# Layer 1 of a two-layer transformer kernel: the experts of the mixture run on their own tokens in 64 sorted tiles instead of on all tokens

## The reference

```python
def _L1_attn_ref(x, ...):            # 16 heads, 128 score features (64 plain, 64 with rope), 128 value features
    scores = g * sem_scores + (1.0 - g) * geo_scores
    attn = jax.nn.softmax(where(causal, scores, NEG_INF), axis=-1)      # 1024 x 1024 per head
    return einsum('bhqk,bkhd->bqhd', attn, v).reshape(b, sl, H * DV) @ wo

def _L1_ffn_ref(hidden_states, ...):
    topk_w, topk_idx = jax.lax.top_k(softmax(x @ gate_w.T), 4)          # 4 of 32 experts for each token
    comb = zeros((T, 32)).at[arange(T)[:, None], topk_idx].add(topk_w / sum(topk_w))
    out0 = sigmoid(x @ shared_expert_gate_w.T) * (silu(x @ sg.T) * (x @ su.T)) @ sd.T   # 512 hidden
    def body(acc, inp):                                                  # for each of the 32 experts
        gu = x @ gu_w.T                                                  # 2 * 96 hidden
        h = silu(gu[:, :96]) * gu[:, 96:]
        return acc + w_e[:, None] * (h @ dn_w.T), None
```

## Time and profile before

| | us |
|---|---|
| median of 3 runs (1105.45 to 1122.83) | 1106.43 |
| the profiled execution, its own time | 1106.36 |
| its span, first to last instruction | 1104.6 |
| layer 1 from its first instruction, 308.4, to the end | 796.2 |
| transposes of head 0 to transposes of head 15 | 680.9 |
| mean granted TensorE clock, share of full speed | 0.929 |

### The profile page before, as it was taken

One profiled execution on the slowest core, in us unless ns is written; L12 is line 12 of the kernel. 1 busy time (PEld: TensorE's weight loads), 2 busy tenths in 40 slices (PEclk: granted clock), 3 DMA queues, 4 the chain that ended last, 5 costly groups with the idle time before them and its releaser, 6 DMA issues.

```text
span 1104.6 us, 15520 instructions
## 1 busy us (share of the span) xinstructions
PE 988.5 (89%) x5701; PEld 753.1 (68%) x5701; DVE 792.2 (72%) x1338; ACT 477.2 (43%) x981; POOL 401.8 (36%) x352
## 2 busy tenths in 40 slices
PE   4797999977777879999999999999999999999996
PEld 3684544533644758787787787777878778777775
DVE  5687555630558568868968868877896896987883
ACT  3322554553232344444544535545444453453552
POOL 2430000010034344635525535454463452544441
PEclk9895588786889989999999999999999999999999
DMA  5630121100030210200200020020020020001000
GB/s 223 229 88 1 31 60 31 32 1 1 21 110 16 60 46 10 68 25 1 56 22 25 11 67 25 10 67 25 11 67 25 1 52 25 25 10 49 15 1 38
DMA packets 19452, 46.41 MB, mean 42 GB/s; under 512 B 3033, under 2 KB 4705, under 8 KB 19105
## 3 DMA queue, kind: packets, MB, share of 16 engines
q1 hardware_dynamic: 19376, 45.43, 13.6%
HBM read 37.81 MB, written 7.61 MB: 41 GB/s over the span
## 4 chain that ended last, share of the span: by engine, by line
PE 50%; DVE 16%; issue 3%; DMA 1%; ACT 1%; POOL 0%; SPq 0%; DVEq 0%; ACTq 0%
PE bank L1535 15%; PE bank L1571 10%; PE bank L1662 8%; PE bank L1581 8%; PE bank L1639 4%; PE bank L1557 4%; DVE d_pT_lo L1421 3%; DVE d_swap L1281 2%; DVE d_swap L1283 2%; DVE d_g_act L1260 1%; DVE d_neg_max L1308 1%; DVE d_rot L1281 1%; DVE d_rot L1296 1%; DVE d_g_act L1256 1%; DMA d_vw_raw<-in_w_v 1%
## 5 line engine op out<-in xcount | busy, mean ns | idle before, releaser
L1471 POOL TENSOR_SCALAR d_probs<-d_probs,d_row_inv 128x1024 f32<-128x1024 f32 (+7 forms) x128 | 101.4, 794 | 227.0 <-DVE d_row_inv L1313 226.5
L1160 ACT ACTIVATE d_probs<-bank,d_neg_max 128x1024 f32<-128x1024 f32 (+7 forms) x128 | 95.5, 746 | 96.5 <-DVE d_neg_max L1308 93.9
L598 DVE TENSOR_REDUCE b_maxes<-bank 128x2 f32<-128x1024 f32 (+2 forms) x96 | 89.5, 956 | 37.3 <-PE bank L626 20.4
L1421 DVE TENSOR_TENSOR d_pT_lo<-bank,d_pT_hi 128x512 fp32r<-128x512 f32 x192 | 98.5, 547 | 21.1 <-ACT d_pT_hi L1217 13.6
L1217 ACT CAST d_pT_hi<-bank 128x512 fp32r<-128x512 f32 x192 | 84.9, 483 | 65.7 <-PE bank L1639 65.0
L1535 PE MATMUL bank<-xT_hi,d_gu_hi 128*128 128x512 f32 x224 | 97.0, 433 | 9.8 <-DVE d_g_act L1256 5.6
L1308 DVE TENSOR_REDUCE d_neg_max<-bank 128x1 f32<-128x1024 f32 (+7 forms) x128 | 95.1, 748 | 11.3 <-PE bank L1584 11.1
L1639 PE MATMUL bank<-ident,d_probs 128*128 128x128 f32 x576 | 83.0, 277 | 17.7 <-DVE d_pT_lo L1421 15.9
L575 ACT ACTIVATE b_probsT<-bank 128x512 f32<-128x512 f32 x140 | 76.0, 593 | 48.6 <-PE bank L626 40.2
L1535 PE MATMUL bank<-xT_hi,d_gu_lo 128*128 128x512 f32 x224 | 90.5, 404 | 0.0
L1535 PE MATMUL bank<-xT_lo,d_gu_hi 128*128 128x512 f32 x224 | 90.4, 403 | 0.0
(11 more groups left out here) (238 smaller groups left out, 2544.9 us busy)
## 6 DMA issues: line engine op xcount, KB each, us to landing
gu_raw<-in_gu SPq DMA_DIRECT2D x24, 256.0 KB, 2.6
d_cb<-comb_scratch SPq DMA_DIRECT2D x9, 512.0 KB
qk_raw<-in_w_qk SPq DMA_DIRECT2D x16, 256.0 KB, 6.3
d_ow_raw<-in_ow_b SPq DMA_DIRECT2D x8, 384.0 KB, 3.2
q_stack<-a_part_hi SPq DMA_DIRECT2D x4, 512.0 KB, 5.4
k_stack<-a_part_hi SPq DMA_DIRECT2D x4, 512.0 KB, 5.1
d_vw_raw<-in_w_v SPq DMA_DIRECT2D x8, 256.0 KB, 10.3
d_ow_raw<-in_ow_a SPq DMA_DIRECT2D x8, 256.0 KB, 10.2
```

The source lines that it names most:

```text
L598: nc.vector.tensor_reduce(maxes[:, p % 2, c, :, i], bank[:, first:first + 2, 0:w], AX_X, ALU.max, negate=True).then_inc(maxed, 1)
L1160: nc.scalar.activation(probs[s % NP_][:, 0:width(s)], score_bank(s, width(s)), ACT.Exp, bias=neg_max[:, h.col(s)], accum_out=row_sum[:, h. ...
L1421: nc.vector.tensor_tensor(pT_lo[c][:, j:j + blocks, col:col + P], bank[:, T_BANK + tu % 2, 0:blocks * P].rearrange("p (b q) -> p b q", b=b ...
L1471: nc.gpsimd.tensor_scalar(probs[s % NP_][:, 0:width(s)], probs[s % NP_][:, 0:width(s)], row_inv[:, h.col(s)], 1.0, ALU.mult, ALU.mult).the ...
```

## The change

**Experts.** Each token has 4 experts, so there are 4096 pairs of token and expert, called slots here. Slots are sorted by expert, each expert's padded to whole tiles of 128, in 64 tiles (`XTILES`) of which each belongs to one expert. `rank` on PE and a longer routing on DVE (18 pieces, `routes`) compute the slot of each token and the expert of each tile. POOL scatters the normed token rows into a memory buffer (`x_slots`, 8192 rows) with 32 indirect DMAs of 128 rows. Two tiles at a time (`PAIRS` = 32) then go through four units: `X` turns the rows (4 transposes), `G` is gate and up (12 matmuls of 192 columns), `H` turns the hidden tile (2 transposes), `Y` is down (6 matmuls of 256 columns). DVE steps of a pair are `xlo`, two for the gate, `hlo`, `yout`; results go to `y_slots` in memory. At the end POOL gathers them with 32 more indirect DMAs, and DVE adds them with their weights (`combine`). Weights of a tile's expert (`ew`, 128 x 640) are loaded by SP, which reads the expert's number from memory into a register first (`value_load`), and are split by ACT and POOL.

**Layout.** `acc` has tokens on the partitions. An output unit is two token tiles of 3 matmuls of 256 columns. `join_layer0` no longer turns `x` or the gate, and stores the normed rows (`x_normed`, 1 MB). `x_slots` (8 MB) is cleared in `project_layer0` by 8 DMAs of 1 MB on SP's queue, behind the loads of the first pair of heads and ahead of those of pairs 1 and 2.

**Shared feed-forward and routing.** They move from the prologue into heads 0 and 1 as units `sg` (gate, up) and `so` (down). The prologue keeps `qk` and `v` of the first heads and two score tiles. Heads 2 to 14 hold the 32 pairs: 3 in each even head but head 2, which has 2, and 2 in each odd head. Head 15 holds none.

**Order.** A class `Plan` replaces the lists. It puts the fillers (`sg`, `so`, `rank` or `X G H Y`) evenly between the steps of `ORDER` by its own costs and gives every PE step a time; the steps of DVE, ACT, POOL and SP are sorted by such times plus fixed lags. The numbers in it are the program's own and nothing measured here.

```diff
@@ -279,6 +290,11 @@
+            sp.wait_ge(zeroed, 1)
+            slots = scratch["x_slots"].rearrange("(n p r) d -> n p r d", n=CLEARS, p=P)
+            for n in range(CLEARS):
+                sp.dma_start(slots[n], zeros.rearrange("p (o d) -> p o d", o=1).to_broadcast([P, NT, D])
+                             ).then_inc(early["cleared"], 16)
...
+            sp.wait_ge(norm.step, norm.DONE + NT)
+            sp.dma_start(scratch["x_normed"].rearrange("(j p) d -> p j d", p=P), xn[:]).then_inc(xn_stored, 16)
+            sp.wait_ge(xn_stored, 16)
...
+class Plan:
...
+    FILL = {1: (0.0, 0.8), 2: (0.3, 1.0)}
+    ORDER = ("T0 S2 S3 T1 S4 T2 S5 qk0 S6 T3 S7 qk1 T4 qk2 T5 pv0 qk3 T6 T7 S8 pv1 S9 "
+             "out0 v0 out1 v1 out2 v2 out3 v3")
...
+        return {"qk": 1.4, "v": 1.44, "out": 0.72, "sg": 1.4, "so": 1.44, "rank": 1.0, "X": 0.45, "G": 1.2, "H": 0.23,
+                "Y": 0.75}[name]
...
+    def fillers(self, h):
+
+        if h < 2:
+            pairs = [("sg", (p, part)) for p in range(4 * h, 4 * h + 4) for part in range(2)]
+            outs = [("so", (h, n)) for n in range(OUT_UNITS)]
+            return pairs[:6] + ([("rank", ())] if h == 0 else []) + pairs[6:] + outs
+        return [(name, (q,)) for q in EXPERT_PAIRS[h] for name in "XGHY"]
...
+            while k < len(fill) and done >= (first + (last_at - first) * (k + 0.3) / len(fill)) * total:
+                self.add(*fill[k])
+                k += 1
+            self.add(*step)
+            done += self.cost(*step)
...
-    PE_ORDER = [
-        "T0 S2 pair0 S3 T1 S4 pair1 T2 S5 qk0 S6 S7 T3 pair2 qk1 T4 T5 qk2 pv0 qk3 T6 T7 S8 pv1 S9 "
-        "out0 out1 out2 out3",
-        "T0 S2 S3 pair0 T1 pair1 S4 S5 qk0 T2 S6 pair2 T3 S7 qk1 qk2 T4 T5 pv0 T6 qk3 T7 S8 pv1 "
-        "out0 v0 v1 S9 v2 out1 out2 v3 out3",
-    ]
...
+    def expert_steps(lead):
+
+        free = END("so", 1, OUT_UNITS - 1) + 13.2 - lead
+        return [(max(START("G", i // 2) - lead + 2 * (i % 2), free + 1.2 * i), "ew", (i,)) for i in range(2 * NQ)]
...
+    dve_order = ordered(
+        after("S", 0.1, "max") + after("S", 2.6, "inv") + after("T", 0.7, "tlo") + after("qk", 0.1, "rope")
+        + after("v", 0.8, "vlo") + after("pv", 0.8, "pvlo") + after("out", 0.1, "oadd") + after("so", 0.1, "soadd")
+        + [(t + 0.3, "spair", (at[0],)) for t, _, at in after("sg", 0, "") if at[1] == 1]
+        + after("X", 0.8, "xlo") + after("G", 0.7, "gate") + after("H", 0.6, "hlo") + after("Y", 0.1, "yout")
+        + [(ROUTE_AT + ROUTE_GAP * n if n < 7 else max(ROUTE_AT + ROUTE_GAP * n, END("rank") + 0.1 + 1e-3 * n)
+            if n < 13 else END("rank") + ROUTE_GAP * (n - 12), "route", n) for n in range(ROUTE_FUNCS)]
+        + [(COMBINE_AT + 6 + 3.2 * j, "combine", j) for j in range(NT)])
...
+                + expert_steps(13)
+                + [(max(t, END("so", 1, OUT_UNITS - 1) + 1 + 2 * at[0]), name, at) for t, name, at in ahead("X", 8, "xs")] + after("Y", 1.0, "ystore")
+                + [(COMBINE_AT + 100 + n, "store", j) for n, j in enumerate(STORED)])
...
+                    i = at[0]
+                    if i == 0:
+                        sp.wait_ge(unit_done, done("so", 1, OUT_UNITS - 1))
+                        sp.wait_ge(scattered, NT * TOPK * 16)
+                    if i >= 2:
+                        sp.wait_ge(ew_hi_done, i - 1)
+                        sp.wait_ge(ew_lo_done, i - 1)
+                    e = sp.value_load(scratch["slot_expert"][0:1, i:i + 1], min_val=0, max_val=NE - 1)
+                    sp.dma_start(ew_raw[i % 2], d["ew"][bass.ds(e, 1)].rearrange("o p n -> (o p) n")
+                                 ).then_inc(ew_in[i % 2], 16)
...
+                    j = at
+                    dve.wait_ge(gathered[j], TOPK * 16)
+                    for k in range(TOPK):
+                        dve.wait_ge(acc_done, acc_at[name, at] + k)
+                        nc.vector.scalar_tensor_tensor(acc[:, j, :], yk[:, (j % NYK) * TOPK + k, :], top_w[:, j, k:k + 1],
+                                                       acc[:, j, :], ALU.mult, ALU.add).then_inc(acc_done, 1)
+                    dve.wait_ge(acc_done, acc_at[name, at] + TOPK)
+                    nc.vector.sem_inc(combined)
...
+                elif name == "scatter":
+                    j = at // TOPK
+                    if at == 0:
+                        pool.wait_ge(xn_in, 16)
+                        pool.wait_ge(route_step, SLOT_STEP + 1)
+                        pool.wait_ge(early["cleared"], CLEARS * 16)
+                    nc.gpsimd.indirect_dma_start(scratch["x_slots"], bass.IndirectOffsetOnAxis(slot_u[:, at:at + 1], 0),
+                                                 xn[:, j, :], None).then_inc(scattered, 16)
+                else:
+                    j, k = at // TOPK, at % TOPK
+                    if at == 0:
+                        for i in range(2):
+                            pool.wait_ge(y_stored[i], 16 * (NQ // 2))
+                    if k == 0 and j >= NYK:
+                        pool.wait_ge(combined, j - NYK + 1)
+                    nc.gpsimd.indirect_dma_start(yk[:, (j % NYK) * TOPK + k, :], None, scratch["y_slots"],
+                                                 bass.IndirectOffsetOnAxis(slot_u[:, at:at + 1], 0)
+                                                 ).then_inc(gathered[j], 16)
...
+                elif name == "G":
+                    q = at[0]
+                    pe.wait_ge(unit_free, freed("X", q))
+                    pe.wait_ge(ew_lo_done, 2 * q + 2)
+                    for a in range(2):
+                        out = unit_bank(u)[:, a * GW:(a + 1) * GW]
+                        for k in range(KT):
+                            slots = slice((k * 2 + a) * P, (k * 2 + a + 1) * P)
+                            cols = slice(k * GW, (k + 1) * GW)
+                            hi, lo = ew_hi[q % 2][:, a, cols], ew_lo[q % 2][:, a, cols]
+                            for n, (m, w) in enumerate(three((xs_hi[:, slots], hi), (xs_lo[:, slots], hi),
+                                                             (xs_hi[:, slots], lo))):
+                                last = nc.tensor.matmul(out, m, w, start=(k == 0 and n == 0),
+                                                        stop=(k == KT - 1 and n == 2))
```

1434 lines of the change are left out of this document (777 added, 657 removed), and 8 rows, old and new, of tables (ACT_ORDER, DVE_ORDER).

## The result

| | before | after |
|---|---|---|
| median, us | 1105.94 (4 runs, 1102.66 to 1122.83) | 1206.71 (4 runs, 1203.57 to 1222.29) |
| ratio | | 1.091 (95% interval 1.087 to 1.095) |
| span of the profiled execution | 1104.6 | 1205.3 |
| first transposes (T0) of head 0, from the span's start | 381.7 | 341.1 |
| heads 0 and 1 | 100.8 | 151.0 |

The account below looks back on a forecast made before the run. PE was taken to set the rate, DVE next, with DVE setting each head's first part. Prologue −45.7, heads 0 and 1 +15.6, heads 2 to 14 −15, tail +12, layer 0 0: −33, so 1073 us (−3.0%), range 1025 to 1118.

Parts of the forecast that it names:

- 64.4 stay: Heads 2 to 14: removing the old experts' 25.2 us of PE from a round of 89.6 leaves 64.4.
- DVE loses three pairs, 7.2, so 15.4 stay: Even head, T0 to pv0: removing three old expert pairs' DVE steps shortens this part from 22.6 us to 15.4.
- the third rope ahead of pv0: Even heads: with G between qk2 and pv0, pv0 waits for the third rope, +3.5 us; T0 to pv0 stays 22.8.
- Price of a pair: Heads 2 to 14: each pair of expert tiles adds 2.97 us on PE, 0.2 of it for a type change.
- Waits of 2 to 2.3 us: Second part of a head, after pv0: pairs' units add waits of 2.3 us in even heads, 2 in odd ones.
- Heads 0 and 1: Shared feed-forward, routing and scatters moved here: head 0 +6.4, head 1 +3.3, POOL's scatters +6, together +15.6 us.
- Prologue: Start of layer 1 up to T0 of head 0: 27.5 us where it was 73.3, a gain of 45.7.
- the clears' cost in PE's wait for pair 1: Layer 0: 8 MB of clears delay pair 1's loads, hidden by 6 us, so 0; +7 at two thirds of the rate.
- The tail: T0 of head 15 to the end: 32 gathers on POOL at 1.2 us each make 42.0 into 54, +12.
- Rival 1: Heads 2 to 14: experts fill the waits, rounds reach PE's sum of 81 us, total 1035; chance 0.25.
- Rival 2: POOL's 64 indirect DMAs wait behind DVE at 2.25 us each, total 1140; at 3.1 each, 1195; chance 0.15.
- Rival 3: G's and Y's narrow matmuls take 0.2 us for 0.115, clears run slower, clock may drop; total 1098; chance 0.15.

Follow-up runs that it names:

- before_no_pairs: Kernel before without the experts' pairs in its 16 heads, hand order otherwise kept; heads 2 to 14 took 496.6 us for 580.1, a round 74.8 to 78.4.
- no_pairs: Changed kernel without the experts' tiles, gathers and combination; routing, scatters and shared feed-forward stay; heads 2 to 14 took 551.4 us for 655.2, profiled time 1080.4.
- no_unit_before_pv: Changed kernel with no expert unit between qk2 and pv0 or qk3 and pv1 from head 2 on; 1.127 times the kernel before, heads 2 to 14 678.8 us.
- searched_order: Changed kernel's same work in another order of steps, with some planner lags changed; 1136.2 and 1141.8 us beside 1104.7 for the kernel before, heads 2 to 14 596.4.
- clears_later: Changed kernel with the eight clears issued in layer 0's attention, two after each of four pairs' row maxima; 1.092 times the kernel before.

## Why the prediction was wrong, point by point

The forecast span was 1071.5, the measured one 1205.3. The 134 us fall on the terms of the sum so: layer 0 and prologue 5, heads 0 and 1 35, heads 2 to 14 90, tail 4.

- **"64.4 stay", and in the walk "DVE loses three pairs, 7.2, so 15.4 stay".** This is the step that failed: the old experts' busy time was taken off as if it were all time of the round. The prediction takes off 7.2 in the first part of either head (T0 to pv0) and 2.8 and 5.6 in the second, 22.8 a round. `before_no_pairs` shows 2.8 and 4.5 going in the first parts of even and odd heads (means from head 4 on; even heads keep 19.8 us, not 15.4) and 1.4 and 4.4 in the second, 13 a round and 12.8 over all heads: attention's own handovers between PE, ACT, DVE and POOL, a small part of it at the lower clock, keep 76.4, and the old experts had lain half in its waits. The first part was not DVE's alone either: in head 4 PE is busy for 21.6 of its 22.65 us and DVE for 19.7. What the change puts in was forecast at 21.2 a round and took 24.4; in the changed kernel's order 85 stay without pairs (`no_pairs`).
- **A slip in the sum.** The parts 22.8 and 20.1 make an even head 42.9, not 42: +3.3 for +2.6. So the walk's own figures give −10 for heads 2 to 14 and not −15, and 1078 us. The bounds taken as independent give about 1031 to 1103, not 1045 to 1100. Both leave the forecast on the faster side.
- **Order.** The text compared three places and priced one in heads 2 to 14, the third rope ahead of pv0. It is there, 2.8 us where 3.5 were forecast, but `no_unit_before_pv`, which undoes it, is slower. What cost more was the fourth rope and `xlo` ahead of the low parts that pv1 needs: 34.5 us in 13 heads with pairs, 27.5 without. Beyond it, `searched_order` finds 24 us more. From hand order to the new one attention alone lost 54.8; half of that is not traced to single steps, and the output on token rows may be in it.
- **Price of a pair.** 2.97 of PE forecast (0.2 of it for a change of type, which stands on no row and shows in no run), 3.24 measured, of which 1.9 with nearly no work in the units. "Waits of 2 to 2.3 us" per head were too small: the second part of heads 4 and 5, forecast 20.1 and 25.7, took 24.3 and 30.5, while the first part took 25.3 and 20.2 for 22.8 and 19.4.
- **The balance of the experts.** From T0 of head 0 to the end they cost 722.9-606.3 = 116.6 us in the kernel before and 864.2-740.0 = 124.2 in the changed one, gathers and combination included, routing and scatters not. PE has 202 us of columns less and 95 more, and no time is won by it: this is where the expected gain went. The rest of what is lost behind T0 of head 0 shows without any pairs too, 740.0 for 606.3: 73 in heads 0 and 1, 55 in heads 2 to 14, 6 in the tail.
- **Heads 0 and 1.** Forecast +15.6, measured +50.2. The shared work costs 44.4, not hidden at all; I had added it to one engine's sum in head 1 and to DVE's in head 0, where both engines' times and the waits add up.
- **Prologue.** T0 of head 0 28.1 us after the first instruction of layer 1 (at 313.0), forecast 27.5: right. In the kernel before, that instruction is at 309.7 and not at 308.4, where the gate's last transpose of `join_layer0` still runs; so the prologue gained 43.9 for 45.7, and layer 0, forecast 0, gave +3.3. The clears held SP's issue, and the block's end waits for SP: `clears_later` takes that wait away. The prediction had the clears' cost in PE's wait for pair 1, which does not come.
- **The tail.** +16 for +12: the issue of a gather takes 1.25 from one to the next where 1.2 was taken. Only 8 of the 16 go with the gathers; DVE's additions, of which the sum held only the last four, 1.9 us, are in the 12 us that go besides when there are no pairs.
- **Rival 1** (81 a round) fell. **Rival 2** had the side right, slower, but not the mechanism: neither 2.25 nor 3.1 us for an issue was seen. Scatters took 0.96 to 1.45 us and gathers 0.94 to 1.20, DVE at work or not. The Trainium skill ("SBUF — State Buffer", section "SBUF: two separate sides") would have such a DMA wait while DVE copies from SBUF to SBUF. DVE's 32 large copies here (`yout`) read a PSUM bank, so no run here tests it. **Rival 3**: matmuls of 192 columns kept 0.114 us, so not the price; its clock is there in part, 0.94 in heads 4 to 14 for 0.99 before, some 30 us by the estimate above, and it falls after waits of PE.

The range, 1025 to 1118, left out the case that came: both slow rivals priced an operation, none the loss of cover.

## What to carry to other kernels

Work that is interleaved with a chain of handovers need not be worth its engine time. Before taking it out or replacing it, time the kernel without it: that one number (here 76.4, not 64.4, a round) says what can be won at most. Where two engines are each busy for 70 to 80% and a table or a planner's lags order them, look for the step on which the next long wait rests and for what stands ahead of it in the other engine's queue; one such step was worth 34 us here. A pair's four units cost 1.9 us even with nearly no work in them; whether fewer and larger units would be better was not run. And read the granted clock with the waits: both controls without the pairs ran at a lower clock than the kernels that they stand for (0.94 for 0.99 to 1.00, 0.91 for 0.92 to 0.94), so a part of their time is the clock's.

## What was not expected of the hardware

The issue of eight DMAs of 1 MB in a row held SP for 19.8 us, 2.5 each, where others of its DMAs take 0.3 to 1.6. The size alone does not do it: two of the same clears at a time, in `clears_later`, took 0.7 each. In the changed kernel the DMA engines were at work all through that stretch, at 331 GB/s from 58.0 to 86.0 us (window).

Indirect DMAs of 128 rows cost POOL 1.25 us each from issue to issue, 0.95 of it shown as busy, and land 2.4 (scatters) and 2.8 us (gathers) after, in the median.
